# Filler matmuls and a new order of work in the opening of a fused attention and gated-MLP kernel

## The reference, cut to what matters

```
x  = x + dwconv(x)                      # cpe1: 3 taps along the tokens, per channel
xn = layernorm(x) * g + b               # norm1
act_res = silu(xn @ actp_w + actp_b)    # act_proj
xi = xn @ in_w + in_b                   # in_proj
xi = silu(dwconv(xi)) ...               # then q, k, linear attention, out, a second conv and an MLP
h  = silu(xn0 @ w1 * s1) * (xn0 @ w2 * s2)   # ffn of the first norm xn0; "gates"
h  = gelu(h @ h1 * ..); h = gelu(h @ h2 * ..); return h @ w3 * ..
```

## Time and profile before

| what | value |
|---|---|
| median of 3 executions | 1038.87 us (1038.81 to 1039.82) |
| the profiled execution, its own time | 1038.23 us |
| its span in the profile | 1036.4 us |
| PE busy | 1002.4 us, 97% of the span |
| DVE busy | 747.5 us, 72% |
| ACT busy | 603.1 us, 58% |
| POOL busy | 239.5 us, 23% |
| granted TensorE clock | 1.00 |
| chain that ended last, by engine | PE 68%, DVE 7%, issue 4%, ACT 3%, DMA 2% |
| first slice of 40 (26 us): PE, DVE, ACT, POOL | 3, 6, 4, 3 tenths busy |

### The profile page before, as it was taken

The page is one execution under the profiler, slowest core; times in us unless marked ns, Lnnn a source line. Parts: engine busy times, 40 slices in busy tenths (PEclk is TensorE's granted clock), DMA queues, the critical chain, the costliest instruction groups (busy, mean ns, idle before and its releaser), DMA issues.

```text
span 1036.4 us, 17189 instructions
## 1 busy us (share of the span) xinstructions
PE 1002.4 (97%) x6628; PEld 899.7 (87%) x6628; DVE 747.5 (72%) x965; ACT 603.1 (58%) x875; POOL 239.5 (23%) x221
## 2 busy tenths in 40 slices
PE   3999999999999999999999999999999999999998
PEld 3778877888877788888899889989999999999998
DVE  6874688544537768988876586876878977877664
ACT  4788667667436375556555454555547654665444
POOL 3444245233504100000000131231301322112210
PEclk9999999999999999999999999999999999999999
DMA  8989715868686645534302773325593323222310
GB/s 308 419 249 369 230 51 204 302 195 234 222 331 215 211 139 187 184 102 166 119 22 82 269 259 102 107 77 183 183 384 125 122 82 123 94 83 83 108 42 22
DMA packets 68802, 181.20 MB, mean 175 GB/s; under 512 B 5056, under 2 KB 26176, under 8 KB 65088
## 3 DMA queue, kind: packets, MB, share of 16 engines
q1 hardware_dynamic: 68720, 180.08, 50.1%
HBM read 122.39 MB, written 66.06 MB: 182 GB/s over the span
## 4 chain that ended last, share of the span: by engine, by line
PE 68%; DVE 7%; issue 4%; ACT 3%; DMA 2%; POOL 0%; DVEq 0%; ACTq 0%
PE pr L2293 41%; PE pr L206 13%; PE pr L2489 9%; DMA h_s<-u 2%; DVE xp_lo L2021 1%; PE pr L2440 1%; PE pr L199 1%; PE pr L2271 1%; PE pr L192 1%; ACT u L1446 1%; DVE x L1572 1%; DVE u L2027 0%; PE pr L2433 0%; DVE tf L2005 0%; DVE tf L2009 0%
## 5 line engine op out<-in xcount | busy, mean ns | idle before, releaser
L2293 PE MATMUL pr<-xp_hi,wb 128*128 128x256 f32 x1344 | 315.5, 280 | 2.4 <-DVE u L2027 1.4
L2293 PE MATMUL pr<-xp_lo,wb 128*128 128x256 f32 x1344 | 314.9, 279 | 0.0
L2293 PEld LDWEIGHTS pr<-xp_hi,wb 128*128 128x128 f32 x1344 | 252.1, 188 | 4.5 <-issue 4.4
L2293 PEld LDWEIGHTS pr<-xp_lo,wb 128*128 128x128 f32 x1344 | 253.1, 188 | 0.0
L2293 PE MATMUL pr<-u_hi,ring 128*128 128x512 f32 x256 | 102.4, 400 | 1.8 <-POOL u_lo L950 1.0
L2293 PE MATMUL pr<-u_lo,ring 128*128 128x512 f32 x256 | 100.0, 391 | 0.0
L1430 ACT CAST xp_hi<-tf 128x1024 fp32r<-128x1024 f32 x48 | 50.3, 1047 | 56.9 <-PE pr L2293 21.4
L2021 DVE TENSOR_TENSOR xp_lo<-tf,xp_hi 128x1024 fp32r<-128x1024 f32 x48 | 61.9, 1289 | 19.5 <-ACT xp_hi L1430 19.4
L2489 PE MATMUL pr<-wf_hi,h_hi 128*128 128x256 f32 x256 | 74.6, 291 | 0.0
L2489 PE MATMUL pr<-wf_lo,h_hi 128*128 128x256 f32 x256 | 71.6, 280 | 0.0
L2489 PE MATMUL pr<-wf_hi,h_lo 128*128 128x256 f32 x256 | 71.4, 279 | 0.0
(11 more groups left out here) (236 smaller groups left out, 2507.2 us busy)
## 6 DMA issues: line engine op xcount, KB each, us to landing
ring<-w_s SPq DMA_DIRECT2D x42, 512.0 KB, 7.4
uf<-h_s SPq DMA_DIRECT2D x16, 1024.0 KB, 4.9
wb<-s_s SPq DMA_DIRECT2D x8, 1024.0 KB, 9.4
wb<-w_s SPq DMA_DIRECT2D x6, 1024.0 KB, 10.6
vw<-v_s SPq DMA_DIRECT2D x8, 514.0 KB, 6.9
xt<-x SPq DMA_DIRECT2D x8, 512.0 KB, 6.0
xn_s<-xh SPq DMA_DIRECT2D x8, 512.0 KB, 8.9
stage<-w_gated SPq DMA_DIRECT2D x2, 2048.0 KB, 13.5
```

What stands on the lines that cost most here:

```text
L2293: return e.matmul(bank, w.bitcast(dt), v_.bitcast(dt), start=first, stop=last, skip_group_check=True)
```

## The change

On PE: it no longer waits for the parameters first, but for `checked` 1 (POOL has cleared `acc`), and multiplies `acc` by itself five times (512 columns, float32) into `front_bank[2]`, which nobody reads. `keep_running(count)` is new and multiplies the identity by itself (128 columns, float32) into the same bank, `count` times; it stands at five places of the opening, with 8, 3, 3, 22 and 14 products. `offsets_of_weights` is split in two parts, of which one stands ahead of `a_channels(1)`. `in_proj(0)` stands ahead of `a_channels(2)`.

On ACT: `high_of_xg(0)` comes ahead of `copy_xn(1)`; `high_of_norm(0)` ahead of `apply_xn(2)`; `xi_out(0)` ahead of `copy_xn(2)`; and `apply_xn(3)` goes from the opening into step -1, behind the units 0 and 1. On DVE: the first check waits for `a_tr` 1 also, `norm_moments(0)` comes ahead of `xn_moments(2)`, and `xn_moments(3)` goes into step -1, behind `norm_offsets(1)`. On POOL: `low_of_xg(0)` waits for the second side tap of tile 0, and `inverse_deviation(3, "a")` comes behind `inverse_deviation(1, "b")`. On SP: the second group of pieces is issued ahead of tile 2, and the third ahead of tile 3.

```
 SP
-                if n < 2:
-                    load_x(2 + n)
+                if n in (1, 2):
+                    load_x(1 + n)
 POOL
             halo(1, xh, "xh_w", 1, "xh_halo")
+            pool.wait_ge(s["b_taps"], 2)
             low_of_xg(0, xg1_lo, mid(xh[0]), xg1_hi)
             inverse_deviation(0, "b", "b_applied")
             inverse_deviation(2, "a", "a_applied")
-            inverse_deviation(3, "a", "a_applied")
             halo(2, xh, "xh_w", 1, "xh_halo")
             inverse_deviation(1, "b", "b_applied")
+            inverse_deviation(3, "a", "a_applied")
             halo(0, xi, "c_xi", KC, "xi_halo")
 ACT
             copy_xn(0)
             conv1_centre(0)
+            high_of_xg(0, xg1_hi, mid(xh[0]))
             copy_xn(1)
             split_attn_weights()
-            high_of_xg(0, xg1_hi, mid(xh[0]))
             conv1_centre(1)
             apply_norm(0)
+            high_of_norm(0)
             apply_xn(2)
-            high_of_norm(0)
+            xi_out(0)
             copy_xn(2)
-            apply_xn(3)
-            xi_out(0)
             act_out(0)
             for i in P1_STEPS:
                 front("p", i, "first")
+                if i < 0:
+                    apply_xn(3)
 DVE
+            e.wait_ge(s["a_tr"], 1)
             check_staged(range(0, 1))
             conv1_side(0, True)
+            norm_moments(0)
             xn_moments(2)
-            norm_moments(0)
-            xn_moments(3)
             norm_offsets(0, "b", "b_applied")
...
                 if i < 0:
                     norm_offsets(i + 2, "b", "b_applied")
+                    xn_moments(3)
 PE
+            e.wait_ge(s["checked"], 1)
+            for n in range(5):
+                e.matmul(front_bank[2], acc[:, 0:P].bitcast(F32), acc[:, 0:TOK].bitcast(F32), start=True, stop=True)
             e.wait_ge(s["prm_in"], 32)
+            def keep_running(count):
+                for n in range(count):
+                    e.matmul(front_bank[2][:, 0:P], ident[:], ident[:], start=True, stop=True)
...
                 a_channels(0)
+                keep_running(8)
+                offsets_of_weights(0, 1)
                 a_channels(1)
-                offsets_of_weights()
+                keep_running(3)
+                offsets_of_weights(2, 3)
+                keep_running(3)
                 norm_tokens(0)
+                keep_running(22)
                 norm_back(0)
+                keep_running(14)
+                in_proj(0)
                 a_channels(2)
-                in_proj(0)
                 e.wait_ge(s["biased"], 1)
```

More of the change, by code:

```diff
@@ L2192, in chunk, with offsets_of_weights @@
                 return lambda k: buf[:, k, :]
-            def offsets_of_weights():
+            def offsets_of_weights(*parts):
                 e.wait_ge(s["wf_in"], 16)
-                for j in range(2 * KC):
+                for j in parts:
                     for k in range(KC):
@@ L2199, in offsets_of_weights @@
                                         start=(k == 0), stop=(k == KC - 1))
-                last.then_inc(s["offsets"], 1)
+                if j == 2 * KC - 1:
+                    last.then_inc(s["offsets"], 1)
             def a_channels(i):
```

## The result

The changed kernel takes 1044.19 us (median of 6 executions, 1043.28 to 1048.99) where the kernel before, run in turn with it, takes 1039.59 (1038.81 to 1039.90): a ratio of 1.0055, with a 95% interval of 1.0041 to 1.0069. By the ratio that is 5.7 us more, between 4.3 and 7.2; the two medians lie 4.6 apart. The forecast was 1046.0 with a range of 1042.7 to 1048.0, and "slower": right in the sign and in the range, high by 1.8 us. It had started from 1038.87, the median of three earlier executions, so that its increase of 7.1 was high by 1.4.

What follows compares the result with a forecast made beforehand. Prediction: PE bounds the kernel behind 63 us, with DVE nearly as full before. It added +5.8 us for ACT's wait and +1.3 for the clock, +7.1 on 1038.23, plus 0.64 for the median: 1046.0 us, range 1042.7 to 1048.0.

Steps and rivals of the forecast that it cites:

- The opening: Up to `full` of unit 0: `in_proj(0)` ends 3.4 us sooner, of which 0.7 is left on DVE, 1.3 on PE.
- The wait: Step -1: ACT's `apply_xn(3)` waits for POOL's offset and DVE's moments, holding up silu of unit 2; +5.8 us.
- the level: PE after its 5.9 us pause: clock falls to the lower level, slow transposes and unit 4 products; +1.3 us.
- nothing behind 63 us takes it back: Behind 63 us the delay stays whole, as PE's few waits are for engines late by the same amount.
- 0.52 for the fall and 0.35 against it: Clock after PE's pause in step -1: falls, 1046.0 us, chance 0.52; rival, stays up, 1044.7 us, chance 0.35.
- 14 us of waits: PE behind 63 us: 14 us of waits in 973, in pieces of at most 1.0, for DVE, ACT and POOL.
- The wait costs little because the moments are done early: Rival, step -1: ACT's wait for `apply_xn(3)` costs +0 to +2 us, near 1039; chance 0.05.
- the lead of the opening: Rival: the 3.4 us gained at the end of `in_proj(0)` hold past step -1, giving 1035.5 us; chance 0.04.
- Slow fillers: Rival, opening on PE: fillers don't lift the level, `in_proj(0)` begins about 10 us late, near 1050 or more; chance 0.04.
- POOL's chain: POOL in step -1: 1.8 us from first instruction to the end of tile 3's offset, up to 3 possible.

Runs made afterwards that it cites:

- e1: The changed kernel with `apply_xn(3)` on ACT moved behind `high_of_norm(1)` in step -1; 1040.76 us, ratio 1.0020 to the kernel before.
- e8: The changed kernel with `apply_xn(3)` on ACT behind `high_of_norm(1)` and POOL's `inverse_deviation(3)` behind unit 2 in step -1; 1037.83 us, ratio 0.9989 to the kernel before.
- e3: The changed kernel with 22 more filler products on PE, ahead of the up product of unit 3; 1043.08 us, ratio 1.0038 to the kernel before.
- e9: The changed kernel with SP's old order of loads, the tiles ahead of the pieces; 1043.85 us, ratio 1.0048 to the kernel before.
- e7: The changed kernel with `xn_moments(3)` between tile 1's side taps, `inverse_deviation(3)` behind `halo(2)`, `apply_xn(3)` ahead of step -1; 1037.12 us, ratio 0.9975 to the kernel before.
- e6: The e7 kernel with `a_channels(2)` ahead of `in_proj(0)` on PE and `copy_xn(2)` ahead of `xi_out(0)` on ACT; 1036.66 us, ratio 0.9978 to the kernel before.
- e4: The changed kernel without any fillers (the five first products and all `keep_running` calls), its new order kept; 1047.96 us, ratio 1.0090 to the kernel before.

## Why the prediction was right

- **The opening.** `norm_back(0)` at 25.0 was 24.81, `in_proj(0)` at 29.0 was 28.79, the first gate product at 37.7 was 37.41, flag 0 at 35.9 was 35.51, `full` at 41.4 was 40.88. Each came out 0.2 to 0.5 us sooner than counted. DVE's hole behind 32.3 was counted at 2.1 and is 2.25. The ten instructions of the first fillers took 6.16 us, between the two bounds of 4.3 and 8.6, so that they rose from the one level to the other.
- **The wait.** Moments at 46.1 (measured 45.5), offset at 47.9 (47.4), `apply_xn(3)` to 50.0 (49.5), PE from 44.9 to 50.8 (44.8 to 50.1), ended by ACT's silu as said. e1 and e8 show that this is the cause and not only a neighbour: with ACT's wait gone more than half of the loss is gone, with POOL's gone too all of it.
- **The size.** The forecast had +5.8 for the wait and +1.3 for the level, 7.1. Behind the flag it is 5.11 (e3) and 1.56, together 6.67. The wait was counted 0.7 too high, mostly since the lead that DVE brought was 1.28 at `full` 0 and not 0.7; the level 0.26 too low: besides the transposes, the four products ahead of them and five behind were slow. That 1.3 came near 1.56 has luck in it: e9 has the same pause and lost only some 0.6 with the level. By the transposes of 169.89 +6.00 is left, and 5.7 by the ratio. The step "nothing behind 63 us takes it back" failed by this 0.67. It isn't a slack that takes delays up: every changed kernel gains 0.3 to 0.8 us between the flag and that row, the faster ones as well, e7 and e8 by 0.65. The traces show the place: from the first product of `in_proj` at 131.69 (138.33 in the change) to the products of `vt` and `kt` at 141.08 (147.07) it is 9.39 us before, 8.74 in the change and in e8, and the difference is in short pauses of PE. What makes them in the kernel before is open. And of the "14 us of waits" behind 63 us, 4.3 are not waits of that kind but the end of the span behind PE's last product.
- **The clock.** 0.52 for the fall and 0.35 against it was cautious; the fall is shown, by a granted clock of 0.77 in the stretch from 48 to 63 us, by 1.97 for eight transposes, and by e3, in which work in the pause keeps it away. The Trainium skill ("TensorE: Matmul & The Clock Gate", HAM oscillation) warns that waits between bursts send the clock back; the trace agrees, with 0.63 to 0.79 a product behind the 5.37 us where it was 0.39 to 0.48 ahead of them.
- **The rivals.** "The wait costs little because the moments are done early" named the condition, moments done by about 40 us, and e7 fulfils it: then the lead of the opening does hold, though 1.3 us of it behind the flag and not 3.4. "Slow fillers" fell: 44 of them took 5.08 us (4.9 were counted), 28 took 3.29 (3.1).
- **What was missed.** POOL's list. The prediction looked at what ACT's wait holds up, and counted POOL's chain only as something that others wait for. `low_of_u(0)` behind `inverse_deviation(3, "a")` costs 3.2 us by itself (e1 against e8, a fall of the level in it). It changed no number here, because the longer wait covered it; it would have made "put `apply_xn(3)` later" look like the whole cure.

## What to carry to other kernels

Before work is moved out of a slow opening into a dense stage, see on each engine's list what will be queued behind every part of it, ACT's and POOL's parts as well as the one that is moved: here ACT and POOL both waited for the same moments, each with other work behind, and taking away the longer wait only showed the next. Look for an earlier place on the engine that the moved work needs. The change itself had made a hole of 2.25 us on DVE, and the same moments put there, with POOL's and ACT's parts moved forward too, turn +5.7 us into -2.6; the same place did as well when the hole was gone (e6). A stall of PE costs its wait and then the slow products behind it (here 5.1 us, and 0.6 to 1.6), so count both.

## What the runs showed of the hardware

- The level can fall after a pause of 2.53 us, and it falls late. In e1 PE had paused for 0.39 us, run eight transposes, and paused for 2.53; then products ran at full speed again from 49.80 on, three of them, and only from 50.58 to about 54 did they take about 0.6. The granted clock of e1 in pieces of 2 us (the columns are those of the stretches above):

```profile
48.00:50.00 2.00, 0.20 (x1) 0.23 (x2) 1.06 (x2) 0.31 (x1) 2.00 (x2) 1.00 1.39 492
50.00:52.00 2.00, 2.00 (x7) 1.59 (x7) 1.97 (x3) 2.00 (x4) 1.31 (x2) 0.66 0.19 70
52.00:54.00 2.00, 2.00 (x7) 1.54 (x6) 1.52 (x3) 2.00 (x5) 0.00 (x0) 0.50 0.00 0
54.00:56.00 2.00, 2.00 (x15) 1.74 (x13) 1.97 (x2) 1.48 (x3) 1.60 (x2) 0.99 0.37 84
```

- The mean clock of a whole execution doesn't tell how fast PE's products ran. Of e1's 12, the 6 with a mean of 0.998 to 1.000 take 1039.1 to 1040.2 us, and the 6 with 0.995 to 0.997 take 1041.3 to 1043.3. Only one of e1's has a trace (1043.03 us, mean 0.996), and half of what its mean lacks lies behind the start of PE's last product, where nothing but the end of the work is waited for: 6.58 us at 0.69, for 4.56 us at 1.00 in the kernel before (first line e1, second before). Where the other five lost theirs stays open. In e3, with work in the pause, all six have 0.999 or 1.000, and they lie within 1.7 us.

```profile
1034.62:1041.20 6.58, 0.27 (x3) 0.07 (x1) 1.52 (x3) 0.00 (x0) 0.00 (x0) 0.69 0.25 82
1031.84:1036.40 4.56, 0.28 (x3) 0.07 (x1) 1.51 (x3) 0.00 (x0) 0.00 (x0) 1.00 0.36 119
```

- In the first 31 us the column of the granted clock says 1.00 whether eight transposes take 1.97 (before, e4) or 1.09 (the change). There the durations tell the level, not the column; from 48 us on the two agree.
- The first five fillers multiply zeros (`acc` has just been cleared), and they bring the level up all the same: eight transposes at 9.48, the first work behind them and ahead of any product of the identity, took 1.06, where they took 1.94 at 9.53 before.
- DVE's check of half a piece takes 0.69 us when POOL is idle (at 43.05 in the change), and 1.53 at 50.95, beside POOL's subtraction.
